# Probabilities times values in one piece a group instead of three, in a two-layer kernel on one core

## The reference, cut to what matters

```python
c_kv = x @ W_dkv.T                       # 16 heads share it
attn = einsum('bhql,bkl->bhqk', q_lat, c_kv) / sqrt(hs)
attn = softmax(where(causal, attn, -inf))
y_lat = einsum('bhqk,bkl->bhql', attn, c_kv)
y = einsum('bhql,hld->bqhd', y_lat, v_eff)
...
x = x + s * silu(ffn(xn))                # a mixture of 8 experts, top 2
# second layer: a linear recurrence over the tokens (delta rule), gate by x @ sign(W)
```

## Time and profile before

| | |
|---|---|
| median of 3 runs | 621.88 us (619.85 to 626.63) |
| the profiled execution | 621.56 us, of which the span is 619.8 |
| granted clock of PE, mean | 0.994 of full speed |
| PE busy | 578.6 us (93%) |
| DVE busy | 391.4 us (63%) |
| ACT busy | 353.0 us (57%) |
| POOL busy | 171.3 us (28%) |
| first piece of `pv`, rounds 0, 3, 4 | at 65.86, 260.50, 329.79 us |

### The profile page before, as it was taken

The page is one execution under the profiler, slowest core; times in us unless marked ns, Lnnn a source line. Parts: engine busy times, 40 slices in busy tenths (PEclk is TensorE's granted clock), DMA queues, the critical chain, the costliest instruction groups (busy, mean ns, idle before and its releaser), DMA issues.

```text
span 619.8 us, 17493 instructions
## 1 busy us (share of the span) xinstructions
PE 578.6 (93%) x7289; PEld 387.4 (62%) x7289; DVE 391.4 (63%) x975; ACT 353.0 (57%) x679; POOL 171.3 (28%) x335
## 2 busy tenths in 40 slices
PE   7789989899998999899998999899999999899897
PEld 3445655576575866676666766676666776565465
DVE  4478685757658676858668676848667575411553
ACT  4322466755666466756676566746675566666231
POOL 7156122403214221423214221432224200501121
PEclk9899999999999999999999999999999999899999
DMA  4765193747253005410262015410262000000001
GB/s 118 157 155 126 26 96 87 165 59 65 63 116 75 24 20 122 96 44 2 66 129 74 12 28 114 96 43 4 78 112 70 2 12 1 24 20 2 3 3 35
DMA packets 58163, 39.42 MB, mean 64 GB/s; under 512 B 17957, under 2 KB 57988, under 8 KB 58084
## 3 DMA queue, kind: packets, MB, share of 16 engines
q1 hardware_dynamic: 58051, 38.29, 30.7%
q10 hardware_dynamic: 32, 0.01, 0.0%
HBM read 24.46 MB, written 9.96 MB: 56 GB/s over the span
## 4 chain that ended last, share of the span: by engine, by line
PE 70%; DVE 16%; issue 5%; ACT 5%; POOL 3%; DMA 1%; SPq 0%; DVEq 0%; POOLq 0%
PE ps_v L950 10%; PE ps_s L930 9%; PE ps_a L865 5%; DVE cand L1458 5%; PE ps_e L911 5%; PE ps_a L851 4%; PE ps_c L1015 3%; PE ps_e L738 3%; PE ps_a L820 3%; PE ps_e L903 2%; PE ps_e L907 2%; PE ps_s L933 2%; PE ps_c L997 2%; PE ps_c L1100 2%; DVE stats L1378 2%
## 5 line engine op out<-in xcount | busy, mean ns | idle before, releaser
L1458 DVE TENSOR_REDUCE cand<-ps_s 128x4 f32<-128x512 f32 (+1 forms) x320 | 212.6, 685 | 63.5 <-PE ps_s L933 44.3
L1252 ACT ACTIVATE prob<-ps_e 128x512 f32<-128x512 f32 x320 | 188.8, 599 | 89.6 <-PE ps_e L911 53.9
L930 PE MATMUL ps_s<-kst,qst 72*128 72x128 bf16 (+2 forms) x1024 | 125.1, 234 | 12.5 <-DVE cand L1458 9.1
L930 PEld LDWEIGHTS ps_s<-kst,qst 72*128 72x128 bf16 (+1 forms) x1024 | 72.0, 98 | 72.3 <-DVE cand L1458 38.9
L911 PE MATMUL ps_e<-qst,kst 75*128 75x256 bf16 (+3 forms) x416 | 104.6, 282 | 0.0
L950 PE MATMUL ps_v<-prob,vaug 128*32 128x512 f32 (+3 forms) x1024 | 89.0, 444 | 0.0
L903 PE MATMUL ps_e<-identb,negmask 128*128 128x150 bf16 (+3 forms) x320 | 72.7, 227 | 8.6 <-ACT prob L1252 8.5
L907 PE MATMUL ps_e<-qst,kst 128*128 128x128 bf16 x384 | 74.4, 220 | 0.0
L911 PEld LDWEIGHTS ps_e<-qst,kst 75*128 75x128 bf16 x416 | 40.6, 98 | 3.5
L903 PEld LDWEIGHTS ps_e<-identb,negmask 128*128 128x128 bf16 x320 | 31.2, 97 | 18.4 <-ACT prob L1252 14.2
L738 PE MATMUL ps_e<-identb 128*128 128x512 bf16 x115 | 40.0, 402 | 1.9 <-POOL identb L520 1.9
(11 more groups left out here) (340 smaller groups left out, 932.5 us busy)
## 6 DMA issues: line engine op xcount, KB each, us to landing
qst<-q_scratch SPq DMA_DIRECT2D x48, 192.0 KB
kst<-k_scratch SPq DMA_DIRECT2D x48, 192.0 KB
q_scratch<-qparts SPq DMA_DIRECT2D x24, 128.0 KB, 2.3
k_scratch<-kparts SPq DMA_DIRECT2D x24, 128.0 KB, 2.3
x_res<-in_L_attn_x_dram SPq DMA_DIRECT2D x8, 256.0 KB, 3.3
xn<-in_L_attn_x_dram SPq DMA_DIRECT2D x7, 256.0 KB, 3.4
out_dram<-second SPq DMA_DIRECT2D x7, 256.0 KB, 2.4
max_scratch<-mrow SPq DMA_DIRECT2D x16, 96.0 KB, 1.8
```

What stands on the lines that cost most here:

```text
L930: last = mm(ps_s[:, bank, w * n:w * (n + 1)], q[0:rows, hd, tok(i)], k[0:rows, hd, keys[0]:keys[1]], start=(n == 0), stop=True, skip_group ...
L1252: af(prob[:, u, :], ps_e[:, u % 2, :], ACT.Exp).then_inc(S["e_emptied"], 1)
L1458: vec.tensor_reduce(cand[:, i, h0:h0 + FILLS * (len(hds) - 1) + 1:FILLS, S_SLOT[u]], ps_s[:, u % 2, :].rearrange("p (a c) -> p a c", a=len ...
```

## The change

`PLAN` names one step `pv` where `pv2` stood, and `pv0` and `pv1` are gone from it (`LAST_PLAN` keeps the three). The merged step runs the same 16 matmuls in the same order. As the first units of a group are now read after the first units of the next group have been written, `prob` gets 14 slots instead of 10: units 0 to 3 of odd groups go to slots 10 to 13. `pv_used` counts groups instead of pieces, and ACT's exponential waits for it at units 0 and 4 only. In slots (4, 1) to (4, 3) the steps are put into another order as well.

```diff
+SLOTS = 14
...
-    (3, 9): ["pv1", "c_u2"], (4, 0): ["m_parts1", "gelu", "stacks1"], (4, 1): ["pv2", "c_y2"], (4, 2): ["v"], (4, 3): ["yt", "x1", "c_r3"],
+    (3, 9): ["c_u2"], (4, 0): ["m_parts1", "gelu", "stacks1"], (4, 1): ["v", "c_y2", "pv"], (4, 3): ["c_r3", "yt", "x1"],
...
-        prob = sb("prob", [P, UNITS, 512])
+        prob = sb("prob", [P, SLOTS, 512])
...
+        def slot(grp, u):
+
+            return u if u >= HEADS // GROUPS or grp % 2 == 0 else UNITS + u
...
-            def pv(b, grp, piece):
+            def pv(b, grp, pieces):
-                if piece == 0:
+                if 0 in pieces:
...
-                pe.wait_ge(S["e_emptied"], b.count(GROUPS * UNITS, UNITS * grp + (4, 8, 10)[piece]))
-                for j, u0, at in (((0, 0, 0),), ((1, 4, 0), (3, 4, 384)), ((2, 8, 0),))[piece]:
+                pe.wait_ge(S["e_emptied"], b.count(GROUPS * UNITS, UNITS * grp + (4, 8, 10)[pieces[-1]]))
+                for j, u0, at in sum((((((0, 0, 0),), ((1, 4, 0), (3, 4, 384)), ((2, 8, 0),))[piece]) for piece in pieces), ()):
...
-                last.then_inc(S["pv_used"], 1)
+                if 2 in pieces:
+                    last.then_inc(S["pv_used"], 1)
...
-                after(act, S["pv_used"], b.count(3 * GROUPS, 0))
+                after(act, S["pv_used"], b.count(GROUPS, 0))
...
-                if u in (0, 4, 8):
-                    after(act, S["pv_used"], cur.count(3 * GROUPS, 3 * (grp - 1) + u // 4 + 1))
-                af(prob[:, u, :], ps_e[:, u % 2, :], ACT.Exp).then_inc(S["e_emptied"], 1)
+                if u in (0, 4):
+                    after(act, S["pv_used"], cur.count(GROUPS, grp - 1 + u // 4))
+                af(prob[:, slot(grp, u), :], ps_e[:, u % 2, :], ACT.Exp).then_inc(S["e_emptied"], 1)
```

More of the change, by code:

```diff
@@ L61 @@
     (0, 0): ["c_u3"], (0, 1): ["gb0"], (0, 2): ["ln2_stats", "c_y3"], (0, 4): ["gb1", "ln2_rstd", "hn_norm"],
-    (0, 6): ["pv0", "gb2"], (0, 7): ["c_ht", "xn2_norm", "rn", "c_out"], (0, 8): ["gb3"], (0, 9): ["pv1", "c_kt", "c_qt"],
-    (1, 0): ["load_x", "m_rows1", "c_xn2t"], (1, 1): ["c_vk", "out"], (1, 2): ["c_gram", "pv2"], (1, 3): ["logits"],
[6 rows of a table removed]
+    (0, 6): ["gb2"], (0, 7): ["c_ht", "xn2_norm", "rn", "c_out"], (0, 8): ["gb3"], (0, 9): ["c_kt", "c_qt"],
+    (1, 0): ["load_x", "m_rows1", "c_xn2t"], (1, 1): ["c_vk", "out"], (1, 2): ["c_gram", "pv"], (1, 3): ["logits"],
[6 rows of a table added]
 }
@@ L99 @@
 PLAN_OLDER = ("c_u3", "c_y3", "c_out")
-PLAN_CURRENT = ("gb0", "gb1", "gb2", "gb3", "out", "pv0", "pv1", "pv2", "yt", "x1", "m_rows1", "zero_state")
+PLAN_CURRENT = ("gb0", "gb1", "gb2", "gb3", "out", "pv0", "pv1", "pv2", "pv", "yt", "x1", "m_rows1", "zero_state")
 SEQUENCES = 8
@@ L950, in pv @@
                         last = mm(ps_v[32 * hh:32 * hh + 32, P * j:TOK], vaug[:, j, head_of(grp, hh), :],
-                                  prob[:, u, o:o + TOK - P * j], start=(j == 0 and grp % FILLS == 0),
+                                  prob[:, slot(grp, u), o:o + TOK - P * j], start=(j == 0 and grp % FILLS == 0),
                                   stop=(j == 2 and grp % FILLS == FILLS - 1), skip_group_check=True)
-                last.then_inc(S["pv_used"], 1)
+                if 2 in pieces:
+                    last.then_inc(S["pv_used"], 1)
             def yt(b, grp):
@@ L1256, in pv @@
                     return
-                act.wait_ge(S["pv_used"], b.count(3 * GROUPS, 3 * grp + 3))
+                act.wait_ge(S["pv_used"], b.count(GROUPS, grp + 1))
                 copy(yT[:, :], ps_v[:, :]).then_inc(S["v_emptied"], 1)
@@ L1316, in _ @@
             pieces = {"xnt": xnt, "q": lambda b: split_hi(b, 0), "k": lambda b: split_hi(b, 1), "v": v, "gates": gates, "gt": gt,
-                      "gelu": gelu, "out": out_piece, "m_rows0": lambda b: m_rows(b, 0), "m_rows1": lambda b: m_rows(b, 1), "pv2": pv, "c_xn2t": c_xn2t, "c_ht": c_ht, "c_kt": c_kt,
+                      "gelu": gelu, "out": out_piece, "m_rows0": lambda b: m_rows(b, 0), "m_rows1": lambda b: m_rows(b, 1), "pv": pv, "pv2": pv, "c_xn2t": c_xn2t, "c_ht": c_ht, "c_kt": c_kt,
                       "c_qt": c_qt, "c_gram": c_gram, "c_ffn": c_ffn}
@@ L1469, in pv @@
                 if grp == GROUPS - 1:
-                    dve.wait_ge(S["pv_used"], b.count(3 * GROUPS, 3 * grp + 3))
+                    dve.wait_ge(S["pv_used"], b.count(GROUPS, grp + 1))
                     vec.tensor_copy(yT[:, :], ps_v[:, :]).then_inc(S["v_emptied"], 1)
@@ L1599, in _ @@
                       "q": lambda b: split_rest(b, 0), "k": lambda b: split_rest(b, 1), "logits": logits, "gates": gates, "gate_norm": gate_norm,
-                      "out": out_piece, "m_parts0": lambda b: m_parts(b, 0), "m_parts1": lambda b: m_parts(b, 1), "pv2": pv, "yt": yt, "c_vk": c_vk, "c_gram": c_gram, "c_ffn": c_ffn, "x1": x1_piece, "early_out": early_out}
+                      "out": out_piece, "m_parts0": lambda b: m_parts(b, 0), "m_parts1": lambda b: m_parts(b, 1), "pv": pv, "pv2": pv, "yt": yt, "c_vk": c_vk, "c_gram": c_gram, "c_ffn": c_ffn, "x1": x1_piece, "early_out": early_out}
             for c in range(NC):
```

4 lines of the change are left out of this document (2 added, 2 removed), and 10 rows, old and new, of the table PLAN.

## The result

The changed kernel takes 657.45 us (median, 649.87 to 658.67), the kernel before 620.87 beside it: ratio 1.056, 95% interval 1.051 to 1.061. It is slower, as forecast, but by 36.6 us where 12.8 were worked out, and outside the range of 622 to 642. The profiled execution took 656.77 us, with a span of 655.0 against 619.8 and a mean granted clock of 0.948 against 0.994. Lines behind the edited functions have moved by 5 or 6: the pieces are L955 now (L950 before), the scores L935 (L930), the maxima L1464 (L1458).

A forecast was written before the change was run, and what follows sets the result against it. PE was taken as the bound (70% of the span), with DVE setting the pace in places. Five full rounds at 2.5 us more plus 0.3 gave 12.8 us, so 634.3 us; range 622 to 642.

The forecast's parts named there:

- the steps: Slot-by-slot prices in a full round: 3.7 us won, 6.2 lost, so 2.5 us more a round.
- the free places: Slots (0, 6), (1, 6), (2, 9): removing a piece wins 0, since PE then waits for DVE or POOL.
- the open ones: Slots where removing a piece wins time: +1.0 at (0, 9), +1.0 at (1, 9), +0.8 at (2, 6), +0.9 at (3, 6).
- the loss of about 1.1 at the turn: Slots (3, 9) to (0, 2), round to round: yt, x1 and DVE's stats come later, -1.1 us.
- Rivals 1 and 2: 1: only saved joints count, 7.3 us faster, chance 0.07. 2: some zero places still win, about 627, chance 0.16.
- The merged piece: Three pieces run as one: 2.31 us, from 1.00 + 1.00 + 0.57 less 0.13 for each of two joints.
- the rule on draining: Skill rule: switching tiling mode drains the array, so each of 56 removed joints would be a saving.
- gt: Two slots after (1, 6): gt stays where it is, waiting about 1.2 us for POOL, so 0 won.
- lev_a6: Slot (3, 1): lev_a6 waits about 1.0 us for DVE's low_blocks, so (2, 9) wins 0, at most 0.1.
- The ends: Round 0 loses 0.3 us; round 6, the first pass and the last pass are priced at 0.
- the third rival: Added waits in slots (0, 5) and (0, 7) lower PE's clock: 3 to 11 us more, 637 to 645, chance 0.10.
- the argument against it: Against a falling clock: the fourth round already has some 3 us of waiting at a granted clock of 1.00.

The follow-up runs named there:

- the filled kernel: Changed kernel plus 17 unread matmuls a round where PE waits for DVE, at (0, 5), (0, 7), (1, 7) and (1, 8): 636.79 us, ratio 1.023.
- group 3 alone: Kernel before with 14 slots, only group 3's pieces merged and the turn of the round in the new order: 626.98 us, ratio 1.010.
- the version between the two: Kernel before with 14 slots; groups 0, 1 and 3 keep the first piece and join second to third: 620.32 us, ratio 1.000.

## Why the prediction was right and wrong

**Right: the direction and the steps.** With the waits filled, a full round is 71.87 us at a clock of 1.00 (71.69 where only (0, 5) and (0, 7) are filled); 71.8 was forecast. The table above shows the parts: the free places at (0, 6), (1, 6) and (2, 9), the open ones at (0, 9), (1, 9), (2, 6) and (3, 6), and the loss of about 1.1 at the turn are borne out as sums by groups, group 0 a little cheaper than thought. The whole kernel, filled, takes 636.8 us, where the sum said 634.3. Rivals 1 and 2 fall: neither the joints alone nor a gentler round is what the full-clock rounds show.

**The merged piece** was forecast at 2.31 and measured at 2.29 to 2.30, so the joint of first and second piece saves as much as that of the rows. The forecast says that the trace agrees with the rule on draining about the size of the joint; the rule came with no size, so the 0.13 us stands on the trace alone.

**gt:** the forecast wait of 1.2 us for POOL isn't there. It waits 0.23, as before, because its time is lost earlier, 0.70 at (1, 7) and 0.48 at (1, 8) for DVE; with its own 0.23 together 1.4. The microsecond was rightly priced at 0, but the place was wrong, and that mattered, since waits there meet with the clock. lev_a6's 0.95 is as forecast (1.0), though the trace doesn't name DVE for it.

**The ends:** in the filled kernel the piece of round 1's slot (1, 2) comes at 137.13 instead of 138.59: 1.5 earlier, where 0.7 would follow from the terms. From the one of round 6 to the end it is 634.0 - 496.89 = 137.1 us against 619.8 - 485.69 = 134.1, so 3.0 more where 1.0 was in the sum. Part of the 2 us is a wait of the last pass, which was priced at nothing; in the changed kernel, timeline of PE:

```profile
570.12 0.39 PE L863 MATMUL ps_a<-gT,pick 96*128 96x512 bf16 x1 [1.07 <-DVE hid L1448]
```

**Wrong: the clock, the third rival.** The sum of 12.8 us prices every slot at full clock: the term for the clock was put at nothing. As a rival the mechanism was written down and given a chance of 0.10 and 3 to 11 us; it held, and cost 20.7 (measured by filling both places). Three parts of the step failed.

First, the argument against it. "The fourth round has some 3 us of waiting and a granted clock of 1.00" compared the waits of a whole round. It passed over how long the single waits are and how close they stand. Before, slots (0, 2) to (0, 7) hold 0.70, 0.82 and 0.22 us, with work between them. After, 1.89 and 1.24 stand 2.8 us apart. The forecast itself had both: "PE would now wait some 1 to 2 us each". Two waits in neighbouring slots, each longer than any of a full round of before, was the sign to weigh most; it isn't needed, as single waits of 1.89 and 1.46 us also had falls behind them (group 3 alone; the version between the two).

Second, the size. The rows of before offered one stretch of 3.5 us, and it was halved, to 1.8 us, as the worst. Now the stretches are mostly 6.8 us long, and they reach past the part where DVE is the pace into c_kt and c_qt. With a fall behind (0, 5) a round takes 74.22, without one 71.69: 2.5 us, against at most 1.8. The window of the changed kernel's round with that stretch alone, and of one with both (the stretch in (1, 7) of round 3, then that of (0, 5) of round 4):

```profile
217.03:291.25 74.22, 67.54 (x907) 49.49 (x906) 48.30 (x120) 43.58 (x83) 19.41 (x34) 0.95 0.26 59
...
291.25:367.07 75.82, 70.54 (x907) 51.94 (x906) 48.38 (x120) 43.51 (x83) 19.43 (x34) 0.91 0.26 58
```

The stretches don't all cost the same. From the scores of (0, 5) to the piece in (1, 2) it is 361.60 - 344.41 = 17.19 us in the kernel filled at (0, 5) and (0, 7). In round 3 of the changed kernel, where the clock falls behind the wait, it is 291.25 - 271.55 = 19.70. In round 4 it falls in the wait itself, and it is 367.07 - 348.08 = 18.99, so 1.8 more instead of 2.5. PE in the filled kernel, then in round 4 of the changed one:

```profile
344.41 0.39 PE L941 MATMUL ps_s<-kst,qst 72*128 72x256 bf16 x2 [0.37 <-DVE cand L1470]
...
348.08 0.59 PE L935 MATMUL ps_s<-kst,qst 72*128 72x256 bf16 x2 [1.88 <-DVE cand L1464]
```

Third, the places. Only (0, 5) to (0, 7) were asked; (1, 7) and (1, 8) cost 5 to 7 us more by the filled runs.

The Trainium skill, page "TensorE: Matmul & The Clock Gate", section "Terms", prices throttled time at the share of pulses withheld, so half of it here. The changed kernel's ten stretches make 64.6 us, by that rule an estimate of 32 us; the runs show 20.7, and the rows just shown say why: part of a stretch lies beside DVE's work. So in this kernel, where another engine sets the pace for a while, the rule is an upper bound. It couldn't have mended the forecast, which halved its one stretch in the same way; the number and the length of the stretches were what it lacked.

## What to carry to other kernels

Work that "costs nothing" because another engine is waited for may still be what keeps TensorE's clock up. Before such work is taken out of a stretch, look at the waits that will stand there alone or side by side, and price a fall of the clock past the end of the shadow, round after round. To tell a lower clock from a real dependency, fill the waits with matmuls that nobody reads: if the kernel gets faster with more work, it was the clock. And a term for the clock is added to the sum of the steps; it isn't an alternative to it.

## What was unexpected of the hardware

The granted clock fell in or after waits that are short against the stretch that follows. A wait of 1.88 or 1.89 us in a stretch where PE was otherwise busy was enough in four of the five rounds that had it, both with group 3 merged alone and with group 0 in three pieces. One of 1.46 us was enough in two of five (the version between the two), 0.82 and 1.24 us two slots apart in three of five, and the pair in slots (1, 7) and (1, 8), 0.70 and 0.48 us in most rounds, in three to five of seven. The stretches in rounds 0 to 6 were 3.4 or 6.8 us, twice 10.2, in all kernels of this study. The same waits, in the same slots, lowered the clock in one round and not in the next: in the kernel with groups 1 and 2 merged, it fell in rounds 1, 4 and 5 and not in rounds 2, 3 and 6. What decides this was not settled. Single executions spread with it: 641 to 653 us with group 0 in three pieces, where the kernel with both places filled kept within 2.4 us (635.9 to 638.3). The kernel before spreads too, from 618.9 us at a mean clock of 0.999 to 628.4 at 0.988.
